# A deformable-convolution kernel: the order of row copies, stores and regrouping around its offset stage, and a new layout of the x offsets' parts

## The reference, cut to what matters

```
x = x + L0(group_norm(x))     # two 3x3 convolutions of 16 channels, each scaled by a sigmoid attention map
x = x + L1(group_norm(x))     # modulated deformable 3x3 convolution, batch norm, relu

offs  = conv3x3(v, offset_w, offset_b)           # 18 maps: y and x offset of each of 9 taps
mask  = 2 * sigmoid(conv3x3(v, mod_w, mod_b))    # 9 maps
sampled[c, k, h, w] = bilinear(v[c], h + ky + off_y[k], w + kx + off_x[k]) * mask[k]
out   = einsum('nckhw,ock->nohw', sampled, w)
```

## Time and profile before

| | |
|---|---|
| Median of three runs | 423.75 us |
| The profiled execution | 425.59 us |
| Its span, first to last instruction | 423.8 us |
| TensorE, VectorE, ACT, POOL busy | 313.0, 319.8, 252.8, 204.3 us |
| Mean granted TensorE clock | 0.905 of full |

### The profile page before, as it was taken

The page is one execution under the profiler, slowest core; times in us unless marked ns, Lnnn a source line. Parts: engine busy times, 40 slices in busy tenths (PEclk is TensorE's granted clock), DMA queues, the critical chain, the costliest instruction groups (busy, mean ns, idle before and its releaser), DMA issues.

```text
span 423.8 us, 14386 instructions
## 1 busy us (share of the span) xinstructions
PE 313.0 (74%) x6057; PEld 203.1 (48%) x6058; DVE 319.8 (75%) x625; ACT 252.8 (60%) x380; POOL 204.3 (48%) x242
## 2 busy tenths in 40 slices
PE   0079999848747419899989989898998999870470
PEld 0022334312213106777757777677775777760460
DVE  5456267833689852999979999799999799993266
ACT  1023322405047108888888888788888888880355
POOL 9770000199491001666646665556666466656000
PEclk9999999969679558999999999999999999996565
DMA  7799200178580643300011001001100000000005
GB/s 226 131 234 239 48 2 0 26 212 235 128 208 9 128 97 90 97 28 3 29 29 44 6 28 28 29 11 40 29 29 26 4 5 3 3 4 19 2 0 198
DMA packets 18106, 28.65 MB, mean 68 GB/s; under 512 B 6890, under 2 KB 7465, under 8 KB 18029
## 3 DMA queue, kind: packets, MB, share of 16 engines
q1 hardware_dynamic: 12397, 19.40, 17.1%
q0 software_dynamic: 2400, 5.07, 5.2%
q10 hardware_dynamic: 3246, 3.27, 3.5%
HBM read 8.03 MB, written 5.83 MB: 33 GB/s over the span
## 4 chain that ended last, share of the span: by engine, by line
PE 42%; ACT 28%; DVE 8%; DMA 7%; SPq 6%; issue 5%; ACTq 1%; POOL 1%; DVEq 1%; POOLq 0%
ACT hx L931 17%; PE ps L641 10%; PE ps L771 9%; ACT zreg L1014 8%; PE ps L584 6%; PE ps L605 5%; PE ps L654 4%; DMA hx<-xpad 3%; SPq L440 3%; PE ps L595 2%; SPq L345 2%; ACT zreg L999 2%; PE ps L780 1%; DMA x_sb<-in_x 1%; DVE x_sb L1397 1%
## 5 line engine op out<-in xcount | busy, mean ns | idle before, releaser
L561 POOL TENSOR_TENSOR prod<-prod 128x416 f32<-128x416 f32 x128 | 134.9, 1075 | 119.4 <-DVE prod L1311 119.4
L1311 DVE TENSOR_TENSOR prod<-ps,hy 128x480 f32<-128x480 f32 (+1 forms) x256 | 137.6, 600 | 23.7 <-PE ps L780 20.9
L780 PE MATMUL ps<-zreg,hx 64*64 64x96 f32 x4608 | 113.1, 247 | 0.0
L931 ACT ACTIVATE hx<-ps 128x576 f32<-128x576 f32 x131 | 78.2, 648 | 49.2 <-PE ps L771 28.5
L780 PEld LDWEIGHTS ps<-zreg,hx 64*64 64x64 f32 x4608 | 101.0, 132 | 7.5
L1018 ACT ACTIVATE hx<-hx,rbias 128x1152 f32<-128x1152 f32 x64 | 81.1, 1267 | 0.0
L1319 DVE TENSOR_REDUCE areg<-prod 128x32 f32<-128x448 f32 x128 | 72.7, 608 | 0.5 <-POOL prod L561 0.4
L641 PE MATMUL ps<-preg,sel 26*128 26x288 bf16 x260 | 42.4, 281 | 31.0 <-ACT zreg L1014 18.1
L771 PE MATMUL ps<-wzp,sreg 128*128 128x144 bf16 x512 | 43.1, 227 | 0.0
L641 PEld LDWEIGHTS ps<-preg,sel 26*128 26x128 bf16 x260 | 19.9, 91 | 46.5 <-issue 31.0
L1014 ACT ACTIVATE zreg<-ps 128x576 f32<-128x576 f32 x64 | 42.1, 658 | 0.0
(11 more groups left out here) (178 smaller groups left out, 354.9 us busy)
## 6 DMA issues: line engine op xcount, KB each, us to landing
scratch<-zreg SPq DMA_DIRECT2D x12, 240.0 KB, 4.2
sreg<-scratch SPq DMA_DIRECT2D x12, 192.0 KB, 2.5
out<-x_sb SPq DMA_DIRECT2D x8, 256.0 KB, 2.1
x_sb<-in_x SPq DMA_DIRECT2D x3, 512.0 KB, 4.9
areg<-xpad POOLq DMA_DIRECT2D x23, 66.0 KB, 3.6
areg<-xpad SPq DMA_DIRECT2D x23, 66.0 KB, 2.7
sreg<-scratch SPq DMA_DIRECT2D x4, 336.0 KB, 3.3
zreg<-xpad POOLq DMA_DIRECT2D x15, 66.0 KB, 4.1
```

What stands on the lines that cost most here:

```text
L561: pool.tensor_tensor(slots[:, :, 0:2 * moved], slots[:, :, 0:2 * moved], slots[:, :, 2 * KEPT:6 * KK], ALU.add).then_inc(folded, 1)
L780: return pe.matmul(g_ps(g, h)[u * W:(u + 1) * W, k - TAPS[h][0], :, :], hx[s, (t + u) % 4, k, :], z_sb[s, y + u + k // 3:y + u + k // 3 + ...
L931: act.activation(hx[:, t % 4, :, :].rearrange("p k (h x) -> p h k x", h=2), dist_ps(bank).rearrange("p h (k x) -> p h k x", k=KK), ACT.Abs)\
L1311: mul = vector.tensor_tensor(pv[:, n0:n1], gv, wv[:, n0:n1], ALU.mult)
```

## The change

Eight edits, which are made together:

1. SP: the rows of chunks 6 and 7 come ahead of the second store, not behind it.
2. SP: the third store comes behind the first load and quarter 2's regrouping, and directly ahead of the fourth store.
3. Quarter 2 is regrouped by two queues: taps 0 to 4 from SP, taps 5 to 8 from ACT. The wait for earlier regroupings (`px_ready`) stands at the calls; ACT has one too, ahead of its four DMAs and of `offsets(3)` and `save_parts(3)`. ACT's `save_parts(2)` moves ahead of them.
4. SP waits for the fourth store ahead of its second loaded piece, not ahead of the last.
5. ACT: the wait for the first three stores ahead of the lead rows is gone; the wait for all four moves from t = 8 to t = 6.
6. VectorE: the four pieces of its image split are made one after the other directly behind the normalisation. Each used to stand ahead of its quarter's x offsets.
7. `parts` has the taps innermost (y, part, image, tap), where it was (y, tap, part, image). So one tap's twelve rows in `tpart` lie nine partitions apart.
8. POOL: the three DMAs of the position planes come behind the rows of chunk 2 of stage 1, not ahead of chunk 0.

```diff
+        def regroup_offsets(eng, q0, q1, taps=range(KK)):
+            n = 2 * CH_ROWS * W
+            g, at = q0 // 2, q0 % 2 * n
+            eng.wait_ge(tp_saved, q1 + CREDIT)
+            for k in taps:
+                eng.dma_start(px[g * NXP:(g + 1) * NXP, k, at:at + (q1 - q0) * n],
+                              tpart[ds(k, NXP, step=KK), q0 * n:q1 * n]).then_inc(px_ready, 16)
...
             store_parts(0)
-            rows_for(4, 5)
+            rows_for(4, 5, 6, 7)
             store_parts(1)
-            rows_for(6, 7)
-            regroup_offsets(0, 2, 0)
+            regroup_offsets(sync, 0, 2)
+
+            sync.wait_ge(off_ready, NCH)
+            sync.wait_ge(xparts_stored, 16 * B * 2)
+            load_piece(0, 0)
+            sync.wait_ge(px_ready, 16 * (1 + PX_DMAS))
+            regroup_offsets(sync, 2, 3, range(0, SYNC_TAPS))
             store_parts(2)
-
-            sync.wait_ge(off_ready, NCH)
-            sync.wait_ge(xparts_stored, 16 * B * (NQ - 1))
-            load_piece(0, 0)
-            regroup_offsets(2, 3, PX_DMAS)
             store_parts(NQ - 1)
-            regroup_offsets(3, 4, 2 * PX_DMAS)
+            sync.wait_ge(px_ready, 16 * (1 + 2 * PX_DMAS))
+            regroup_offsets(sync, 3, 4)
+            sync.wait_ge(xparts_stored, 16 * B * NQ)
...
             save_offsets(NCH - 1)
+            save_parts(NQ - 2)
+            act.wait_ge(px_ready, 16 * (1 + PX_DMAS))
+            regroup_offsets(act, 2, 3, range(SYNC_TAPS, KK))
             offsets(NQ - 1)
-            save_parts(NQ - 2)
             save_parts(NQ - 1)
...
-                act.wait_ge(xparts_stored, 16 * B * (NQ - 1))
...
-                    if t == CH_ROWS:
+                    if t == CH_ROWS - 2:
                         act.wait_ge(xparts_stored, 16 * B * NQ)
...
-                part = [parts[:, rows, :, i, :].rearrange("p y k b -> p y b k") for i in range(NPART)]
+                part = [parts[:, rows, i, :, :] for i in range(NPART)]
```

More of the change, by code:

```diff
@@ L130, in conv_deform_kernel @@
         xrep2 = [xrep_of(v) for v in (xrep_homes[i] for i in (0, 1, 2, 0, 1, 2, 1, 2))]
+        SYNC_TAPS = 5
         REUSES = (None, None, None, 0, 1, 2, 4, 5)
@@ L166, in conv_deform_kernel @@
         parts = areg[:, REP:REP + HH * NPART * B * KK // 2].bitcast(bf16)\
-            .rearrange("p (y k q b) -> p y k q b", y=HH, k=KK, q=NPART)
+            .rearrange("p (y q b k) -> p y q b k", y=HH, k=KK, q=NPART)
         sig = dist[:, 0:2, 0:BANK]
@@ L429, in load_piece @@
                 sync.dma_start(xs_sb[NPART * C:P128, f0:f1], rows[0:C, :]).then_inc(xs_loaded, 16)
-            def regroup_offsets(q0, q1, counted, taps=range(KK)):
-                n = 2 * CH_ROWS * W
-                g, at = q0 // 2, q0 % 2 * n
-                sync.wait_ge(px_ready, 16 * (1 + counted))
-                sync.wait_ge(tp_saved, q1 + CREDIT)
-                for k in taps:
-                    sync.dma_start(px[g * NXP:(g + 1) * NXP, k, at:at + (q1 - q0) * n],
-                                   tpart[k * NXP:(k + 1) * NXP, q0 * n:q1 * n]).then_inc(px_ready, 16)
             def rows_for(*chunks):
@@ L494, in _ @@
             pool.memset(offbc[:, :], 0.0).then_inc(zeroed, 1)
-            pool.wait_ge(attpad_zeroed, 1)
-            for dy in range(3):
-                at = dy * C + NATT
-                pool.dma_start(attrep[at:at + NPOS, 1:1 + H, :].rearrange("p r x -> p (r x)"),
-                               d["pos"][3 * dy * NPOS:(3 * dy + 1) * NPOS, :]).then_inc(pos_loaded, 16)
             for c in range(NCH):
@@ L502, in _ @@
                 replicate(pool, c, POOL_ROWS, xrep, xrep_last)
+                if c == 2:
+                    pool.wait_ge(attpad_zeroed, 1)
+                    for dy in range(3):
+                        at = dy * C + NATT
+                        pool.dma_start(attrep[at:at + NPOS, 1:1 + H, :].rearrange("p r x -> p (r x)"),
+                                       d["pos"][3 * dy * NPOS:(3 * dy + 1) * NPOS, :]).then_inc(pos_loaded, 16)
             def split_low_rows(q):
@@ L675, in parts_quarter @@
                                       parts[:, ds(q * CH_ROWS + i, 1), :, :, :]
-                                      .rearrange("p y k q b -> p (y k q b)"), identh[:, :])
+                                      .rearrange("p y q b k -> p (y q b k)"), identh[:, :])
                 mm.then_inc(tp_ready, 1)
@@ L1224, in split_rows @@
                     vector.wait_ge(split, q * 3 + step)
+                if step == 1 and q:
+                    vector.wait_ge(xparts_ready, q)
                 if step == 0:
@@ L1236, in offsets @@
                 y = q * CH_ROWS
-                for step in range(4):
-                    split_rows(q, step)
                 vector.wait_ge(off_saved, q * 2 + 2)
@@ L1265, in _ @@
             vector.wait_ge(norm2, NCH)
+            for q in range(NQ):
+                for step in range(4):
+                    split_rows(q, step)
             with vector.Fori(0, NQ - 1) as q:
```

2 lines of the change are left out of this document (removed).

## The result

| | before | changed |
|---|---|---|
| Median, 19 runs each | 424.19 us | 422.93 us (416.22 to 425.68) |
| The profiled execution | 425.59 us | 422.93 us |
| Its span | 423.8 us | 421.2 us |
| Mean granted TensorE clock | 0.905 | 0.909 |

A forecast was written before the change was run, and what follows sets the result against it. It took SP's queue of regroupings, store, load and DMA landings before the loop as the bound. Gains 0.7 + 5.6 + 3.0 = 9.3 us, limited to 9.0 by ACT, gave 423.75 - 9.0 = 414.7 us; range 411.3 to 418.8.

The forecast's parts named there:

- priced at nothing, 0.5 us either way: Stage 1: position planes issued behind chunk 2's rows land at 31 us, needed at 40.1; no effect ahead of chunk 0.
- slower: the planes: Rival, stage 1: planes landing late stop TensorE's in-order convolutions; 429 us if they land at 33 us; chance 0.06.
- Term (a): Stage 2, chunk 7's convolution: rows still late behind POOL's third split, low clock; ends at 132.5, gain 0.7 us.
- The far end: Chunk 7's rows landing 4.9 us after the last issue, at 129.4; at the low clock a loss of 0.7 us.
- Term (b): Between the two regroupings: third store and its landing leave SP's path, quarter 2 starts at 143.0; gain 5.6 us.
- Term (c): Quarter 2's regrouping on two queues: SP issues five DMAs instead of nine; gain 3.0 us.
- ACT the later of the tie by 0.4: At the first distance: ACT ready at 149.2, TensorE's result at 148.8, so the gain is 9.0 us instead of 9.3.
- The loop unchanged: In the loop: period stays 3.23 us per pair, with no wait at the fifth pair.
- Edits 6 and 7 at nothing: VectorE's early image splits and quicker writes of the parts: no gain or loss on the path.
- stores behind the loop covered: Stores three and four land by 161.5, second piece at 163.2; needed at the fifth pair, 167.3: 4 us spare.

The follow-up runs named there:

- the two tests: Changed kernel with the position planes' DMAs back ahead of chunk 0: 420.01 us; kernel before with only those DMAs moved behind chunk 2's rows: 428.83 us.
- no_planes: Changed kernel without the three position-plane DMAs and TensorE's wait for them, so the result lacks their part: 420.19 us, ratio 0.9908.
- store_later: Changed kernel with SP's second store behind the first regrouping instead of ahead of it: 426.13 us, ratio 1.0005.

## Why the prediction was wrong, point by point

- **Edit 8, "priced at nothing, 0.5 us either way"**: this is the step that failed most, +3.3 us in the profiled executions, 2.9 and 4.6 by the medians of the two tests by themselves. I asked when the planes would land and found 9 us of room, rightly: TensorE never waits for them. I did not ask what an earlier chunk 0 would meet. It meets attention weights that are not ready, since ACT's square root stands behind sixteen row DMAs (25.78 us, 24.73 before): an idle stretch of 4.08 us, and behind it chunk 1, line 596 and chunk 2 at the low clock. That edit 8 makes the loss is shown by the two tests; this mechanism is read from the waits of the trace. The rival "slower: the planes" had the place right and the mechanism wrong.
- **Term (a), a gain of 0.7**: it was a loss of 0.5. The mechanism held (chunk 7 does not follow chunk 6, POOL's rows are last, the store flies beside them, the clock is low: 4.68 us for the chunk where 4.5 was taken). The size of the landing did not: 4.15 us behind the end of the last issue, some 4.7 behind its start, where I took 3.5. The far end, 4.9 from the earlier trace rows, would have been near. I described the loss and did not count what it was worth to avoid it: 6.4 us for two exchanged lines.
- **Term (b), 5.6**: 5.4 measured; quarter 2 starts 8.56 us behind the first regrouping where 8.4 was worked out; the nine landed in 2.33 us where 2.1 was taken.
- **Term (c), 3.0**: 3.0 measured, twice.
- **ACT the later of the tie by 0.4**: by 0.2. To ACT's save of the first distance the gain of stage 2 was 7.7 us where the prediction had 9.0; the difference is term (a).
- **The loop unchanged**: its period is, its first own pair is not, +1.7 us. The prediction looked at waits in the loop and not at the clock that TensorE brings into it. Which clock that is varied between kernels without a reason that was found, so this part could not have been forecast from the rows; it belonged into the range.
- **Edits 6 and 7 at nothing, stores behind the loop covered**: held. At the fifth pair of the changed kernel nothing waits.
- Together: 3.3 + 1.2 + 1.8 = 6.3 of the 6.4 us between the 9.0 forecast and the 2.6 found in the profiled pair.

## What to carry to other kernels

When work is made ready earlier, look up what the engine behind it is doing at that time, in program order: an operand that comes 5 us sooner to a consumer that is not free gives only an idle TensorE and a low clock. Count for every DMA on the path which instructions stand ahead of it on its own engine, and try the exchange of two lines before rebuilding the queue around it; here it brought 6.4 us up to the first regrouping and 8.7 us by the medians, where the whole change brought 1.3. And where the change shifts TensorE's idle stretches, put the first work behind each of them into the range at both levels of the clock.

## What the runs showed of the hardware that was not expected

- Three loads of 66 KB in four rows each (16.5 KB a row) went out at 19.4 to 20.9 us, in the midst of copies with 32 short rows of the same total size. The DMAs of the core moved 229 to 279 GB/s from 14 to 22 us and 85 to 151 from 22 to 30, at a busy share of 0.99 to 1.15; without the loads they moved 249 to 296 from 22 to 30. Their own landing (median 6.4 us) does not stand out. Without any planes the copies of chunks 3 to 5 land in 4 to 5 us, with the planes there in 9 to 11, and in the kernel before, with the planes at the head, in 8 to 10.
- TensorE, kept busy for 9.7 us by matmuls over 26 partitions, was granted 1.00 in the first of these microseconds and 0.50 from 145 us on; under matmuls over 128 partitions (with other operands) in the same gap it was granted 1.00 throughout.
- SP and ACT issue DMAs side by side at 0.76 and 0.81 us each, with no turn-taking that shows. The issues of the eight row copies of chunks 2 and 3 took 6.0 us on SP and 6.1 on ACT before, 7.1 and 7.3 in the changed kernel, 7.4 and 7.9 in no_planes; the reason was not found.
- Copies landed later beside a large store: POOL's rows of chunk 7 were down 4.15 us behind their last issue with the second store (960 KB) leaving beside them, 1.42 us in store_later without it.
